# A mixture-of-experts layer on one core: expert result rows scattered to a place per token, with 24 result buffers

## The reference, cut to what matters

```
comb = zeros(T, 64).at[arange(T)[:, None], topk_ids].add(topk_w)
act  = silu(g) * u * comb[:, :, None]
routed = einsum('tef,ehf->th', act, w_down)
return x + attn(xn) + routed + shared
```

## Time and profile before

| | |
|---|---|
| median of 3 runs | 293.71 us |
| the profiled execution | 291.93 us |
| its span, first to last instruction | 290.0 us |
| mean granted TensorE clock | 0.959 of full |
| busy: PE, DVE, ACT, POOL | 251.7, 193.6, 164.3, 156.0 us |
| DMA, mean over the span | 232 GB/s, 67.23 MB |

### The profile page before, as it was taken

The page is one execution under the profiler, slowest core; times in us unless marked ns, Lnnn a source line. Parts: engine busy times, 40 slices in busy tenths (PEclk is TensorE's granted clock), DMA queues, the critical chain, the costliest instruction groups (busy, mean ns, idle before and its releaser), DMA issues.

```text
span 290.0 us, 6282 instructions
## 1 busy us (share of the span) xinstructions
PE 251.7 (87%) x1586; PEld 209.7 (72%) x1586; DVE 193.6 (67%) x476; ACT 164.3 (57%) x467; POOL 156.0 (54%) x140
## 2 busy tenths in 40 slices
PE   8978697899999999999999997889999999999000
PEld 6844485799999999999877886779744479999000
DVE  4768936878687786777665756779355469975441
ACT  1378317688887888887666756667445544241000
POOL 4296538755474554744525546311047777777750
PEclk9999979999999999999999999999999999999655
DMA  7999933999999999999889998899163333443330
GB/s 213 321 378 300 292 124 106 346 303 292 288 293 272 308 296 305 293 292 302 301 296 291 306 294 263 279 302 352 59 208 103 93 90 111 128 127 112 109 109 18
DMA packets 35302, 67.23 MB, mean 232 GB/s; under 512 B 6107, under 2 KB 22647, under 8 KB 35264
## 3 DMA queue, kind: packets, MB, share of 16 engines
q1 hardware_dynamic: 29504, 51.49, 55.4%
q0 software_dynamic: 5776, 15.48, 17.4%
HBM read 58.71 MB, written 12.19 MB: 244 GB/s over the span
## 4 chain that ended last, share of the span: by engine, by line
DMA 48%; POOL 15%; issue 11%; DVE 11%; PE 7%; SPq 5%; POOLq 1%; ACT 1%; DVEq 0%; ACTq 0%
DMA w_slab<-in_w 41%; POOL w_split L457 7%; SPq L361 3%; POOL early_w L457 3%; POOL digits L457 2%; DMA digits<-table,gcol 2%; DVE one_hots L767 2%; POOL end_of_ring L457 2%; DMA routed<-early_w 2%; DVE one_hots L777 1%; DMA x_slab<-in_x 1%; PE ps L1138 1%; PE ps L1221 1%; DMA w_split<-routed,key_idx 1%; DVE tab_slab L730 1%
## 5 line engine op out<-in xcount | busy, mean ns | idle before, releaser
L448 POOL DMA_INDIRECT digits<-table,gcol x65 | 71.0, 1093 | 82.3 <-DVE gcol L939 70.7
L1221 PE MATMUL ps<-w_split,xT_both 128*128 128x352 f32 x390 | 88.1, 356 | 6.5 <-ACT xT_both L559 6.3
L1221 PEld LDWEIGHTS ps<-w_split,xT_both 128*128 128x128 f32 x390 | 64.6, 189 | 18.6 <-issue 8.1
L820 DVE TENSOR_TENSOR w_split<-w_ring,w_split 128x704 fp32r<-128x704 f32 x65 | 62.5, 961 | 1.0 <-ACT w_split L553 0.5
L812 DVE SCALAR_TENSOR_TENSOR act_slab<-ps,digits,sg 128x176 f32<-128x176 f32 x64 | 25.6, 399 | 39.7 <-ACT sg L565 36.4
L553 ACT CAST w_split<-w_ring 128x704 fp32r<-128x704 f32 x65 | 51.0, 785 | 0.0
L1249 PE MATMUL ps<-w_ring,act_slab 128*128 128x256 f32 x130 | 38.9, 381 | 0.0
L1250 PE MATMUL ps<-w_slab,act_slab 128*128 128x256 f32 x130 | 38.7, 379 | 0.0
L457 POOL DMA_INDIRECT w_split<-routed,key_idx x24 | 26.1, 1087 | 7.3 <-issue 7.3
L825 DVE TENSOR_TENSOR xT_both<-ps,xT_both 128x256 fp32r<-128x256 f32 x65 | 27.0, 415 | 1.0 <-ACT xT_both L559 1.0
L1250 PEld LDWEIGHTS ps<-w_slab,act_slab 128*128 128x128 f32 x130 | 24.7, 190 | 3.3
(11 more groups left out here) (180 smaller groups left out, 392.0 us busy)
## 6 DMA issues: line engine op xcount, KB each, us to landing
w_ring<-in_w SPq DMA_DIRECT2D x65, 480.0 KB, 4.0
routed<-y SPq DMA_DIRECT2D x33, 128.0 KB
routed<-early_w SPq DMA_DIRECT2D x32, 128.0 KB, 4.4
w_slab<-in_w SPq DMA_DIRECT2D x65, 48.0 KB, 4.8
digits<-table,gcol POOLq DMA_INDIRECT x65, 5.1
x_slab<-in_x SPq DMA_DIRECT2D x4, 256.0 KB, 3.7
table<-tab_slab POOLq DMA_DIRECT2D x1, 1024.0 KB, 8.7
resid<-in_x SPq DMA_DIRECT2D x1, 1024.0 KB, 7.4
```

Of the source, the lines that this page charges most:

```text
L448: pool.indirect_dma_start(out=rows[:, r, :], out_offset=None, in_=table, in_offset=bass.IndirectOffsetOnAxis(ap=gcol[:, r:r + 1], axis=0), ...
L820: V.tensor_tensor(rr(w_lo[:, k % 2, :]), w1_sb[:, k % RING, 0:4 * F], w_hi[:, k % 4, :], ALU.subtract).then_inc(wlo_sb, 1)
L1221: ins = mm(ps[2 + k % 2][:, 0:2 * F], rr(a[:, k % 2, h * P:(h + 1) * P]), rr(b[:, k % (2 if b is w_lo else 4), h * 2 * F:(h + 1) * 2 * F]) ...
```

## The change

- `routed`, `resid` and all keys are gone. DRAM tensor `parts` has 6 rows for each token. Place `p*48 + n` belongs to partition p and the n-th choice in it, counted over its 8 chunks. A running sum over `chosen` (one `tensor_tensor_scan` of 512 elements on VectorE) gives the place, ACT copies it as int16 into 32 more columns of the `table` row, so that a gather brings each row's place with it. A gathered row grows from 1280 to 1408 B.
- VectorE writes a column of places for each tile (`scol`), and GpSimd scatters the tile's result rows by an indirect DMA straight from the result buffer to `parts`. There are 24 result buffers. In the loop GpSimd issues five scatters to eight gathers; 26 scatters come after the last gather.
- SyncE stores no results. It waits for the tile's product (`y_ps`) before it refills the slot.
- `bias_kv` moves from GpSimd to VectorE.
- In the tail SyncE waits for all scatters, then loads each chunk's six rows per token with one DMA (768 KB) and x once more. VectorE's sums lie later in its list, and GpSimd adds the retention output for chunks 0 to 6.
- The loops of ACT and GpSimd over the tiles are written out.

The diff, cut to its core:

```
-    routed = nc.dram_tensor("routed", [(TILES + 1) * P, H], f32, kind="Internal").ap()
-    resid = nc.dram_tensor("resid", [RESID_ROWS, H], f32, kind="Internal").ap()
+    parts = nc.dram_tensor("parts", [T * TOPK, H], f32, kind="Internal").ap()
...
+Y_BUFS = 24
+SCATTER_LAG = 3
+SCATTER_SKIPPED = (1, 4, 7)
...
@@ sync
-                    sp.dma_start(resid[0:T, :].rearrange("(c p) h -> p c h", p=P), x_v).then_inc(resid_done, 16)
-                    sp.dma_start(resid[T:RESID_ROWS, :], x[0:P, :]).then_inc(resid_done, 16)
-                    sp.dma_start(routed[TILES * P:(TILES + 1) * P, :], zero[:]).then_inc(zero_row_out, 16)
-            def store_tile(t, k, row):
-                sp.wait_ge(y_sb, t + 1)
-                sp.sem_inc(sp_waited, 1)
-                sp.dma_start(row, y_bufs[k % Y_BUFS]).then_inc(y_out[k % Y_BUFS], 16)
+            def slot_free(t):
+                sp.wait_ge(y_ps, t + 1)
+                sp.sem_inc(sp_waited, 1)
...
+            sp.wait_ge(y_out[0], n_ov * 16 + y_stores(0))
+            for b in range(1, Y_BUFS):
+                sp.wait_ge(y_out[b], y_stores(b))
+            def load_parts(c):
+                if c >= SUM_CHUNKS:
+                    sp.wait_ge(parts_read, c - SUM_CHUNKS + 1)
+                sp.dma_start(part_sb[c % SUM_CHUNKS], parts_v[:, c, :, :]).then_inc(parts_in[c % SUM_CHUNKS], 16)
+            load_parts(0)
             for n in range(2):
-                sp.dma_start(x_again[:, 4 * n:4 * n + 4, :], resid_v[:, 4 * n:4 * n + 4, :]).then_inc(x_again_in, 16)
+                sp.dma_start(x_again[:, 4 * n:4 * n + 4, :], x_v[:, 4 * n:4 * n + 4, :]).then_inc(x_again_in, 16)
+            for c in range(1, SUM_CHUNKS):
+                load_parts(c)
             for c in range(NC):
+                if c + SUM_CHUNKS < NC:
+                    load_parts(c + SUM_CHUNKS)
...
@@ gpsimd
+            pool.wait_ge(dest16_ready, 1)
             pool.dma_start(table_v[:, :, H:ROW], tab[:, :, H:ROW]).then_inc(table_out, 16)
...
+            def scatter(t):
+                pool.wait_ge(scol_ready, t + 1)
+                pool.wait_ge(y_sb, t + 1)
+                pool.indirect_dma_start(
+                    out=parts, out_offset=bass.IndirectOffsetOnAxis(ap=scol[:, t:t + 1], axis=0),
+                    in_=y_bufs[t % Y_BUFS], in_offset=None, bounds_check=T * TOPK - 1,
+                    oob_is_err=False).then_inc(y_out[t % Y_BUFS], 16)
+            plain, late = E - AHEAD, E - AHEAD + LATE
+            scattered = 0
+            for t in range(late):
+                if t < plain:
+                    fetch(t, t)
+                count = 1 + t % 2 if t >= plain else int(t >= SCATTER_LAG and t % 8 not in SCATTER_SKIPPED)
+                for _ in range(count):
+                    scatter(scattered)
+                    scattered += 1
+            fetch(plain, plain)
+            for t in range(scattered, TILES):
+                scatter(t)
...
-            for b in range(Y_BUFS):
-                pool.wait_ge(y_out[b], y_stores(b))
-            for c in range(NC):
-                gather_parts(c)
+            pool.wait_ge(x_again_in, 32)
+            for c in range(NC - 1):
+                pool.wait_ge(o_sb, c + 1)
+                pool.wait_ge(x_sum, c + 1)
+                G.tensor_tensor(x_again[:, c, :], o_parts[c], x_again[:, c, :], ALU.add).then_inc(res_sb, 1)
...
@@ scalar
+                if n == 3:
+                    act_e.wait_ge(dest_ready, 1)
+                    nc.scalar.copy(tab16[:, :, 2 * (H + E):2 * ROW], dest.rearrange("p (c e) -> p c e", e=E))\
+                        .then_inc(dest16_ready, 1)
...
+                if t >= Y_BUFS:
+                    act_e.wait_ge(y_out[t % Y_BUFS], 16 * (t // Y_BUFS))
+                nc.scalar.copy(y_bufs[t % Y_BUFS], ps[6 + t % 2][:, 0:H]).then_inc(y_sb, 1)
...
@@ vector
+            dve.wait_ge(ex_ready, NC)
+            V.tensor_tensor_scan(dest, flat, flat, c_32("dest_first"), ALU.add, ALU.max).then_inc(dest_ready, 1)
...
+                    V.scalar_tensor_tensor(scol[:, bass.ds(t, 1)], rows16[:, k % AHEAD, bass.ds(t + 2 * (H + E), 1)],
+                                           -1.0, pad[:, bass.ds(t, 1)], ALU.add, ALU.add).then_inc(scol_ready, 1)
...
+                    if k in (9, 17):
+                        bias_kv(i * 2 + (k // 17))
...
-            LAST_SUMS = [[(sum_parts, 0)], [(finish, 0), (sum_parts, 1)], [(finish, 1), (sum_parts, 2)], [(finish, 2), (sum_parts, 3)],
-                         [(finish, 3), (sum_parts, 4)], [(finish, 4)], [(sum_parts, 5), (finish, 5)],
-                         [(sum_parts, 6), (finish, 6)]]
+            LAST_SUMS = [[], [], [0], [1, 2], [3], [4, 5], [6], [7]]
...
-            sum_last()
+            finish(NC - 1)
```

More of the change, by code:

```diff
@@ L24 @@
 SEQ_CHUNKS = 4
-ROW = H + E
+D16 = E // 2
+ROW = H + E + D16
 EXTRA = 1
@@ L37 @@
 UNCHOSEN = 4096.0
-SKIP = 4096
+SKIP = 8192
 SUM_CHUNKS = 5
@@ L210, in build @@
             xn_lo = (xn_lo0, xn_lo1)
-        y_near = sb("y", [P, 4, H])
-        y_bufs = [y_near[:, b, :] for b in range(4)] + [early_w[:, b * H:(b + 1) * H] for b in range(Y_BUFS - 4)]
-        sprod = y_near.rearrange("p (a b) h -> p a (b h)", a=2)
+        y_early = 3 * NG
+        y_bufs = [early_w[:, b * H:(b + 1) * H] for b in range(y_early)]
+        y_table = NC * ROW // H
+        y_bufs += [tab_slab[:, b * H:(b + 1) * H] for b in range(y_table)]
+        product_slab = slab("product_slab", 4 * H)
+        sprod = view(product_slab, 0, 2, 2 * H)
+        y_bufs += [product_slab[:, b * H:(b + 1) * H] for b in range(4)]
         kv = sb("kv", [P, NC, 2 * H])
@@ L227, in build @@
         sgu_sb = sb("sgu_sb", [P, NG, 2 * FS])
-        slab("end_of_hots", 2 * H)
+        end_of_hots = slab("end_of_hots", 3 * H)
+        y_bufs += [end_of_hots[:, b * H:(b + 1) * H] for b in range(3)]
+        assert len(y_bufs) == Y_BUFS
         banks = ctx.enter_context(nc.psum_tensor("ps", [P, 8, 512], f32))
@@ L603, in expert_act @@
                 evac_aT(t, k)
[L605 to L613 removed]
+            for t in range(TILES):
+                expert_act(0, t, ahead=min(3, TILES - 1 - t))
+            for t in range(TILES - 2, TILES):
+                evac_y(t)
             act_e.wait_ge(ov_ready, 1)
@@ L933, in expert_dve @@
                     x_low(t + 2, k)
+                if last and k >= RING:
+                    extra_dest(k % AHEAD, k - RING, link)
+                    V.scalar_tensor_tensor(scol[:, t:t + 1], ov_s[:, 5:6], -1.0, pad[:, t:t + 1], ALU.add, ALU.add)\
+                        .then_inc(scol_ready, 1)
+                else:
+                    V.scalar_tensor_tensor(scol[:, bass.ds(t, 1)], rows16[:, k % AHEAD, bass.ds(t + 2 * (H + E), 1)], -1.0,
+                                           pad[:, bass.ds(t, 1)], ALU.add, ALU.add).then_inc(scol_ready, 1)
                 nxt = fetched_at(k) if last else k
@@ L1077, in _ @@
                 if n == 0:
-                    dve.wait_ge(resid_done, n_ov * 16 + 32)
-                    for b in range(Y_BUFS):
+                    for b in range(y_early + y_table, y_early + y_table + 4):
                         dve.wait_ge(y_out[b], y_stores(b))
```

172 lines of the change are left out of this document (55 added, 117 removed).

## The result

The changed kernel takes 277.87 us in the median of four runs (276.73 to 281.07), the kernel before beside it 294.36. The ratio is 0.946 with a 95% interval of 0.938 to 0.955. Forecast were 278 us, in a range of 269 to 293. The sum is right; three of its terms aren't (the loop, VectorE's line in the tail and the program's end), and their errors nearly cancel.

The account below looks back on a forecast made before the run. Bounds: the loop by full result buffers, stores queued behind weight waits (10.2 us); the tail by GpSimd's 48 gathers. VectorE's end 269.4, plus 6.0 and 1.9, gave 277.3, or 279.1 over the median; forecast 278 us, range 269 to 293.

Parts of the forecast that it names:

- Front, +0.4: Before the loop: VectorE's 512-element scan nearly fits a 1.40 us gap and costs 0.4 us, bounds 0 and 1.3.
- The 10.2 us: Loop: time lost as ACT's result copies wait for stores queued behind weight waits, with 8 buffers; up to 10.2 us free.
- So the loads don't starve PE: Loop: weight loads at a 2.765 us pitch still land about when a never-waiting PE wants them; cost 0.
- GpSimd falls behind, 4.4 us: Loop: 13 indirect DMAs in 8 tiles, some held by VectorE's L820, take 18.5 to 19.8 us; middle cost 4.4.
- rival E: Loop: the shared port is locked for VectorE's whole instruction, last gather at about 238, time about 319 us; chance 0.03.
- The slack of the gathers, 6 us: Loop: gathers go out 13.7 us before PE takes their rows, land in 5.1, wake-ups 2.5; 6 us left.
- Net gain of the loop, 5.4: Loop: 10.2 us freed, less 0.4 for the front and 4.4 for GpSimd, gives 5.4 us.
- Last gather to chunk 0 and x: Tail: last gather at 196.1, 26 scatters at 1.40 us, then loads; chunk 0 and x there at 243.9.
- VectorE's line, 24.3 + 2.5: Tail: after the fourth decay at 242.6, VectorE works 24.3 us, plus 2.5 for GpSimd's adds, to 269.4.
- The end, 6.0: Program's end: from VectorE's last instruction to the span's end go 6.0 us, as before, giving 275.4.
- C: Loop and tail: rival with GpSimd full, scatters at 1.6 to 1.91 us, or new buffers run out; 298 us, chance 0.16.
- D: Loop and tail: rival with a scatter dearer than a gather, from 1.91 us; at 2.3 the time is 323, chance 0.09.

Follow-up runs that it names:

- three loads alone: Three weight loads under way in the loop in place of two: kernel before 282.56 us (0.963); the same edit in the changed kernel 274.37 us (0.945).
- Sixteen buffers alone: The kernel before with 16 result buffers in place of 8, stores and tail as they were: 291.98 us, ratio 0.986.
- the short split: Changed kernel, VectorE's split of the weights cut to 64 of 704 columns from the third tile on: 276.19 us; with three weight loads under way too, 270.19 us.
- the same loop with a last gather behind it: Changed kernel with all retention adds on VectorE and, behind GpSimd's last scatter, a gather into a tile nothing reads: 280.75 us in one run.
- its four variants: The kernel before with 16 buffers (291.98 us), three weight loads under way (282.56), both (282.98), or a last memset on GpSimd (293.56).

## Why the prediction was right in the sum and wrong in its terms

All on the clock of the profiled executions; forecast first.

- **Front, +0.4.** The scan took 1.28 us, within its bounds, and L770 behind it came at 23.47 in place of 23.09: as forecast. VectorE's timeline after:

```profile
22.27 1.28 DVE L767 TENSOR_TENSOR_SCAN route<-chosen,k 128x512 f32<-128x512 f16 x1 [0.20 <-ACT route L545]
23.47 0.66 DVE L770 SCALAR_TENSOR_TENSOR rank_i<-chosen,ps 128x512 int32<-128x512 f16 x1
```

- **What bounds the loop: wrong.** The 10.2 us that it counted as lost there were right in size: three loads alone brought back 9.1 of them (210.77 to 201.66). But the prediction read the copies' waits for stores, saw that the stores stand behind the waits for weights, and still took the buffers for the shortage and wrote that the ring holds loaded weights. Sixteen buffers alone brought 2.4 us of loop, and with three loads 0.2 more than three loads alone (201.47). The root was the wait for the load before last; the full buffers were its shadow.
- **"So the loads don't starve PE": the step that failed.** It kept the pitch of 2.765 us and compared the last load with the loop's end. The need comes earlier: a PE that hardly stalls has the split of tile 63 at 188.13 us, while its weights, out at 187.69 in the changed kernel, need the 4.7 us that the second part of a load took to land (page, median), so they come some 4 us late. By the same rows tile 16's weights are some 19 us early, each tile loses 0.49, and the spare time is gone about at tile 55; with the short split ACT's first wait for weights is that of tile 57, at 175.07. Cost forecast: 0. Measured with GpSimd freed: 207.77 - 199.87 = 7.9 us of loop, 6.0 in the medians. The prediction had named this sign itself, PE waiting for weights after tile 40.
- **GpSimd falls behind, 4.4 us: right in kind and size, but hidden.** A DMA took 1.18 us in the mean from 69 to 190 us (96.5 us for 82), with the issue 1.48; 13 make 19.3 in 8 tiles, between the 18.5 and 19.8 of the bounds. With the weights out of the way the short split brings 203.61 - 199.87 = 3.7 us of loop (6.8 from the other loop end with three loads), and 4.2 in the medians. Up to 1.8 of it may be VectorE's own time, which the short split spares too: the kernel before with three loads has the full split, no scatters and a PE that hardly stalls, and ends its loop at 201.66. Beside late weights the short split brings 0.75 of loop and 1.7 in the medians: of the two limits, freeing GpSimd alone gives little. The Trainium skill (SBUF — State Buffer, "SBUF: two separate sides") says that whichever of the two starts first has the shared port pair for the whole instruction, and that the other fully blocks. The trace agrees on GpSimd's side: of the 97 DMAs from 60 to 205 us, 35 begin inside a split and are longer, all but one, by about what is left of it less 0.1 us; the other 62 take 1.03 us in the mean. It doesn't agree on VectorE's side: the 17 splits that begin within 0.3 us behind the start of a DMA take 0.88 to 0.90 us. The prediction misread this rule: the gather at 182.39 began before L820, so by that rule it was L820 that had to wait, and its 0.89 us show no such wait. Of rival E's 319 us there is no sign.
- **The slack of the gathers, 6 us: right by luck.** No run shows the 2.5 us for wake-ups, and a gather doesn't go out 13.7 us before PE takes its rows: in the kernel before it is 11.3 (72.48 to 83.79 for one of them), which less the 5.1 of the landing leaves 6.2. In the changed kernel the lead falls from 11.1 us for the gather at 72.26 to 5.3 for the one at 160.33, where landing takes 5.5 (page, median): the slack is used up. PE's transposes of their rows, and the second gather:

```profile
83.32 0.38 PE L1196 MATMUL ps<-k,digits 128*128 128x128 f32 x2
...
160.33 1.68 POOL L471 DMA_INDIRECT digits<-table,gcol  x1 [0.30 <-issue]
...
165.59 0.38 PE L1196 MATMUL ps<-k,digits 128*128 128x128 f32 x2
```

- **Net gain of the loop, 5.4.** Measured 2.3 in one execution; the same loop with a last gather behind it ended at 210.95 and gave nothing.
- **Last gather to chunk 0 and x.** 26 scatters at a pitch of 1.44 (35.95 us for 25) where 1.40 was taken; a single one 0.98 to 1.95. SyncE's first load came 1.65 us after the last scatter's end (2.6 forecast, 0.6 of it without a row), x was in 9.2 us later (7.8). All of it lies 4.5 us later than forecast, of which 2.7 came in with the last gather.
- **VectorE's line, 24.3 + 2.5.** Measured 28.8 from the fourth decay's end, of which 1.7 are the waits for chunk 0, x and chunk 1; the remaining 27.1 are the forecast's 26.8. GpSimd's adds took 0.98 us in the mean, not 0.65; they stretched L1030 three times by 0.41 and two pairs of state updates by 0.5 each, 2.2 us in all.
- **The end, 6.0.** Taken over from before as a constant; it was GpSimd's drain, and it fell to 2.6. Unseen luck: -3.4 us.

Sum: the fourth decay ends 2.4 us later than forecast (245.0 against 242.6), VectorE's line is 2.0 longer, the end 3.4 shorter: 276.5 against 275.4.

Of the rivals, C's mechanism is in the trace (GpSimd full, buffers used up) at a scatter of 1.48 us with its issue in the loop and 1.44 behind it, under the 1.6 that it asked for; its price of 298 us belongs to 1.91 and wasn't paid. D is excluded: a scatter costs what a gather costs. From the loop's end to the span's end go 79.2 us before and 68.0 after, and 79.2 and 67.8 with three loads in both: the tail is worth 11.2 us, where the forecast had 9.2. As 3.4 of them are the drain's, which it hadn't seen, what it had in view gave 7.8.

## What to carry to other kernels

Read the chain by line before the waits by engine: where 41% of the span stands behind one load, ask first how many such loads are under way, and try one more. A busy share of the DMA engines near 0.9 doesn't say that they can't move more. And when a stall is read as "buffers run out", ask why the one who frees them is late: twice the buffers in front of the same late worker give back little.

## What the runs showed of the hardware that was not expected

- Two weight loads of 528 KB under way moved 294 GB/s in the loop of the kernel before at a DMA share of 0.94, three of them 348 at 0.99; in the changed kernel 280 at 0.89 and 322 at 0.95.
- GpSimd's drain at the program's end lasts until 9.3 or 9.4 us after its last work in the kernel before and its four variants, and 4.5 to 5.1 in nine profiles of the changed kernel and its variants, after adds, a scatter or a gather alike. What of the program makes the difference is not known; the five have, among other things, GpSimd's loop over the tiles as a loop and 48 gathers in the tail, and no run takes these apart. In all profiles in which GpSimd works nearly to the end, its drain ends last.
